# Convolution unrolled with outputs inside its steps, and the choice of experts moved to GpSimd

## The reference, cut to what matters

```python
# second layer, attention part: h = layernorm(x) * (1 + ca) + sa
z = softmax(einsum('bse,he->bsh', h, W_A) * SCALING, axis=1)      # over the sequence, 16 heads
roll = zp[:, :, (i - j) % S] * tril                               # Toeplitz, causal
v = einsum('bse,fe->bsf', h, W_V).reshape(B, S, 16, 8)
out = einsum('bhij,bjhd->bihd', roll, v)
x = x + ga * (out @ W_O.T + b_O)
# second layer, feed-forward part: h = layernorm(x) * (1 + cb) + sb
logits = einsum('bsh,eh->bse', h, gate_w)
w2, i2 = top_k(softmax(logits), 2)
y = relu(einsum('nh,edh->ned', h, expert_w) + expert_b)           # all 16 experts
x = x + gb * sum(take(y, i2) * w2)
```

## Time and profile before

| | us |
|---|---|
| median of 3 runs (1118.16 to 1122.62) | 1119.12 |
| the profiled execution | 1120.54 |
| its span, first to last instruction | 1118.7 |
| TensorE busy in the span | 1036.0 (93%) |
| VectorE busy | 873.4 (78%) |
| ScalarE busy | 844.8 (76%) |
| GpSimd busy | 672.1 (60%) |

### The profile page before, as it was taken

One profiled execution on the slowest core, in us unless ns is written; L12 is line 12 of the kernel. 1 busy time (PEld: TensorE's weight loads), 2 busy tenths in 40 slices (PEclk: granted clock), 3 DMA queues, 4 the chain that ended last, 5 costly groups with the idle time before them and its releaser, 6 DMA issues. The chain is left out here.

```text
span 1118.7 us, 34142 instructions
## 1 busy us (share of the span) xinstructions
PE 1036.0 (93%) x11851; PEld 712.4 (64%) x11851; DVE 873.4 (78%) x2931; ACT 844.8 (76%) x2678; POOL 672.1 (60%) x1080
## 2 busy tenths in 40 slices
PE   6889998799999998998999999998998889999995
PEld 4667764477777776565577777776565588844442
DVE  4999996588888888665688888887676635299998
ACT  5789984699999998433799999997356866488986
POOL 4999995699888887201798898896233300012222
PEclk9999999999999999999999999999999999999999
DMA  7000000112222211311112122121001452000000
GB/s 241 13 3 12 12 3 1 38 41 67 54 55 49 55 44 44 129 50 35 34 40 59 40 49 50 40 50 43 19 1 40 102 146 80 3 11 15 17 18 19
DMA packets 66499, 50.88 MB, mean 45 GB/s; under 512 B 42262, under 2 KB 53442, under 8 KB 66050
## 3 DMA queue, kind: packets, MB, share of 16 engines
q1 hardware_dynamic: 66339, 48.84, 17.1%
HBM read 21.41 MB, written 2.38 MB: 21 GB/s over the span
## 5 line engine op out<-in xcount | busy, mean ns | idle before, releaser
L1259 PE MATMUL psum<-wa_wqkv,wa_hT 128*128 128x512 f32 x384 | 190.1, 603 | 1.3 <-DVE wa_tmp L1124 1.3
L1216 ACT ACTIVATE wa_p<-psum,wa_nb 128x128 f32<-128x128 f32 x512 | 184.6, 403 | 0.0
L1105 POOL TENSOR_TENSOR wa_p<-wa_p,wa_rrs 128x512 f32<-128x512 f32 x128 | 133.4, 1042 | 10.1 <-DVE wa_rrs L1149 10.1
L1812 POOL TENSOR_TENSOR ex_total<-ex_total,mod 128x128 f32<-128x128 f32 x32 | 15.5, 485 | 205.0 <-DVE ex_total L1940 205.0
L1140 DVE CUSTOM_DVE_ANT_0 psum<-psum,wa_bias 128x128 f32<-128x128 f32 x512 | 132.5, 323 | 6.1 <-PE psum L1297 6.1
L1216 ACT ACTIVATION_READ_ACCUMULATOR wa_p<-psum,wa_nb 128x1 f32 x512 | 124.6, 243 | 0.0
L1987 ACT ACTIVATE cv_z_ex_yw<-psum,ex_w 128x128 f32<-128x128 f32 x384 | 107.0, 400 | 19.8 <-DVE ex_w L1916 7.3
L2058 PE MATMUL psum<-ex_wc,ex_hT 128*128 128x512 f32 x256 | 117.7, 603 | 3.5 <-DVE cv_z_ex_yw L1923 2.1
L1081 POOL TENSOR_TENSOR wa_kr<-wa_kr,wa_tmp 128x512 f32<-128x512 f32 x64 | 81.7, 1277 | 41.6 <-DVE wa_tmp L1124 41.6
L1226 ACT ACTIVATE wa_pT<-psum 128x512 f32<-128x512 f32 x128 | 78.3, 612 | 31.9 <-PE psum L1273 31.7
L1092 POOL TENSOR_TENSOR wa_qr<-wa_qr,wa_rn 128x512 f32<-128x512 f32 x64 | 66.8, 1044 | 57.1 <-ACT wa_rn L1198 57.1
(11 more groups left out here) (264 smaller groups left out, 3026.6 us busy)
## 6 DMA issues: line engine op xcount, KB each, us to landing
wa_vm<-wa_v SPq DMA_DIRECT2D x127, 128.0 KB, 2.4
cv_toep<-cv_zpad SPq DMA_DIRECT2D x32, 136.0 KB, 2.7
cv_toep<-cv_zpad SPq DMA_DIRECT2D x16, 264.0 KB, 4.0
wa_tabs<-in_rotations_dram SPq DMA_DIRECT2D x2, 2048.0 KB, 8.1
wa_rows<-y_rows SPq DMA_DIRECT2D x31, 128.0 KB
wa_rows<-y_rows SPq DMA_DIRECT2D x31, 127.0 KB
x_rows<-in_L_attn_x_dram SPq DMA_DIRECT2D x4, 512.0 KB, 6.1
out_dram<-x_rows SPq DMA_DIRECT2D x32, 64.0 KB, 1.5
```

The costliest lines, as they stand in the source:

```text
L1105: nc.gpsimd.tensor_tensor(p, p, cols_bc(rrs[:, t % 2, r, :], P), ALU.mult)\
L1216: e = nc.scalar.activation(pr[:, t % 2, r, h, :], sim_bank[r][:, P * h:P * h + P], ACT.Exp, bias=nb[:, t % 2, r, h:h + 1], scale=-1.0, acc ...
L1259: nc.tensor.matmul(bank, hT[:, t % 3, :], wqkv[:, INNER * k:INNER * k + INNER], start=True, stop=True).then_inc(done.sem, 1)
```

## The change

The convolution's steps are written out, without a loop. The outputs of the first batch are moved into the second batch's steps: the first turn behind step 4, then in each of steps 5 to 7 the projection of one group and the turn of the next, between the second and the third part; the last projection behind step 7. Rounds 10 to 13 of the set-up go into steps 0 and 1, in the same place. The first six tiles are normalised behind the last step instead of during step 4. ScalarE takes the second batch's exponential, the first `values_now` and `lower_rows` ahead of its last two set-up copies. Copies of the values of groups 3 to 7 move from ScalarE to VectorE. `wog`, `bog` and `mixing` move from VectorE to GpSimd, and GpSimd's bias additions wait for the first batch's probabilities and for rows of step 2. In the experts the five stages of the choice move from VectorE to GpSimd; the comparison is now eight instructions of 128x16 instead of one of 128x128.

```diff
         def phase(gp):
+            def floats(g):
+                v_idx.wait(gp, GT * g)
+                nc.gpsimd.tensor_copy(topf[:, g % 2], topi[:, g % 2, :, 0:2]).then_inc(g_float.sem, 1)
+            def numbers_equal(g):
+                g_float.wait(gp, GT * g)
+                for i in range(GT):
+                    for k in range(2):
+                        m = nc.gpsimd.tensor_scalar(equal[:, g % 2, i, k, :], iota[:, :], topf[:, g % 2, i, k:k + 1],
+                                                    None, ALU.is_equal)
+                m.then_inc(g_equal.sem, 1)
...
+            def weights(g):
+                g_masked.wait(gp, GT * g)
+                v_rec.wait(gp, GT * g)
+                for k in (0, 3):
+                    relu_done[k].wait(gp, GT * (g - 2) + GT - 1)
+                nc.gpsimd.tensor_tensor(w[:, g % 2], chosen[:, g % 2], cols_bc(zrec[:, g % 2], NE), ALU.mult)\
+                  .then_inc(g_w.sem, 1)
-            return Phase([(residual, UP_LAG + 2)], 0, TILES)
+            return Phase([of(floats, 5), of(numbers_equal, 5), of(either, 5), of(masked, 6), of(weights, 6),
+                          (residual, UP_LAG + 2)], 0, TILES)
...
-            return Phase([(relu, UP_LAG), of(z_sum, 6), of(numbers_equal, 5), half[0], of(columns, 2), of(top_values, 4),
-                          of(reciprocal, 6), of(either, 5), of(masked, 6), half[1], of(indices, 4), of(weights, 6),
-                          half[2], of(below_top, 4), of(floats, 4), half[3]], 0, TILES, between)
+            return Phase([(relu, UP_LAG), of(z_sum, 6), half[0], of(columns, 2), of(top_values, 4),
+                          of(reciprocal, 6), half[1], of(indices, 4), half[2], of(below_top, 4), half[3]], 0, TILES,
+                         between)
...
             def relu(t):
-                v_w.wait(dve, t)
+                g_w.wait(dve, t)
...
+                on_gpsimd.mixing(gp)
+                gp.wait_ge(g_w, 2)
                 for g in range(GROUPS):
+                    if g % PER_B == 0:
+                        gp.wait_ge(*((v_rec_prob, 2), (v_lower, parts_done(2, 2)))[batch(g)])
...
+                def values(g):
+                    dve.wait_ge(p_zv, 2 * g + 2)
+                    take_values(nc.vector.tensor_copy, g).then_inc(v_v, 1)
...
-                for r in range(1, SET_BEFORE, 2):
+                for r in (1, 3, 5):
                     on_vector.take(dve, r)
-                for r in range(len(PARTS)):
+                lower_rows(0, 0)
+                for r in (7, 9):
+                    on_vector.take(dve, r)
+                for r in range(1, len(PARTS)):
                     lower_rows(0, r)
-                on_vector.add_bias(dve, 0)
                 probabilities(1)
...
+                    if s < 2:
+                        on_vector.take(dve, SET_BEFORE + 2 * s + 1)
+                    if s in (1, 2):
+                        on_vector.add_bias(dve, s - 1)
+                    if s > QUADS:
+                        g = s - QUADS - 1
+                        residual(g)
+                        on_vector.statistics(dve, g, residual_done)
+                        if g:
+                            on_vector.shift(dve, g - 1)
...
-                for b in range(B):
-                    with pe.Fori(0, QUADS // 2) as j:
-                        for u in range(2):
-                            convolve(j + j + (u + QUADS * b), u)
...
+                for s in range(STEPS):
+                    g = s - QUADS
+                    begin_convolve(s)
+                    for r in range(len(PARTS)):
+                        if r == len(PARTS) - 1:
+                            if g > 0:
+                                o_project(g - 1)
+                                turn_o(g)
+                            if s < 2:
+                                for k in range(2):
+                                    on_tensor.prepare(pe, SET_BEFORE + 2 * s + k)
+                        convolve_part(s, s % 2, r)
+                    if g == 0:
+                        for r in range(SET_BEFORE, SET_ROUNDS):
+                            on_tensor.set_over(pe, r)
+                        turn_o(0)
+                o_project(PER_B - 1)
...
-                for r in range(0, SET_BEFORE, 2):
+                for r in (0, 2, 4):
+                    on_scalar.take(act, r)
+                z_exp(1)
+                values_now(0)
+                lower_rows(0, 0)
+                for r in (6, 8):
                     on_scalar.take(act, r)
                 on_scalar.constants_ready(act)
                 act.sem_inc(a_conv, 2)
...
+                o_columns(PER_B - 1)
+                on_scalar.scale(act, PER_B - 2)
                 keep(STEPS - 1)
+                for step in range(EARLY):
+                    phase.step(step)
```

More of the change, by code:

```diff
@@ L1805, in fill, with mixing @@
             nc.gpsimd.memset(rows[:, :, 0:1], 1.0).then_inc(g_set, 1)
+        def mixing(gp):
+            nc.gpsimd.tensor_copy(pick[...], c.ident[:, :]).then_inc(g_mix, 1)
+            gp.wait_ge(g_mix, 1)
+            nc.gpsimd.memset(pick[0:1, :], -1.0).then_inc(g_mix, 1)
+            gp.wait_ge(g_mix, 2)
+            for b in range(B):
+                nc.gpsimd.tensor_scalar(mix[:, b, 1:P], pick[:, 1:P], c.mod_cols[:, 1, CB, b:b + 1], None, ALU.mult)\
+                  .then_inc(g_mix, 1)
+                nc.gpsimd.tensor_copy(mix[:, b, 0:1], c.mod_cols[:, 1, SB, b:b + 1]).then_inc(g_mix, 1)
         def phase(gp):
@@ new lines, in numbers_equal, with either @@
+            def numbers_equal(g):
[5 more added lines that the diff above has]
+                m.then_inc(g_equal.sem, 1)
+            def either(g):
+                g_equal.wait(gp, GT * g)
+                e = equal[:, g % 2]
+                nc.gpsimd.tensor_tensor(chosen[:, g % 2], e[:, :, 0, :], e[:, :, 1, :], ALU.add)\
+                  .then_inc(g_chosen.sem, 1)
@@ L1995, in experts, with prepare @@
     class Tensor:
-        def prepare(pe, r, bank_left=None):
+        def prepare(pe, r):
             if r == 0:
                 pe.wait_ge(loaded, 16 * LOADS)
[L2000 to L2003, removed]
+            for before in range(r):
+                if set_bank(before) is set_bank(r):
+                    set_done(pe, before)
             bank = set_bank(r)
@@ L2117, in convolution_and_experts, with values_taken, take_values @@
         batch = lambda g: g // PER_B
+        ON_VECTOR = 3
+        def values_taken(eng, g):
+            if g < ON_VECTOR:
+                eng.wait_ge(a_v, g + 1)
+            else:
+                eng.wait_ge(v_v, g + 1 - ON_VECTOR)
+        def take_values(instruction, g):
+            to = vall[:, batch(g), 2 * GT * (g % PER_B):2 * GT * (g % PER_B) + 2 * GT, :]
+            return instruction(to, v_bank[g % 2].rearrange("p (n e) -> p n e", e=HALF))
         side = lambda a: slice(HALF * a, HALF * a + HALF)
@@ L2246, in _ @@
                         keep(s - 1)
-                    if s == QUADS:
-                        for g in range(PER_B):
-                            residual(g)
-                            on_vector.statistics(dve, g, residual_done)
                     if s + 1 < STEPS:
@@ L2253, in _ @@
                             lower_rows(s + 1, r)
-                    if s == QUADS:
-                        for g in range(PER_B):
-                            on_vector.shift(dve, g)
-                later = {9: lambda: on_vector.add_bias(dve, 1)}
+                    if s < 2:
[8 more added lines that the diff above has]
+                            on_vector.shift(dve, g - 1)
+                later = {}
                 for k, g in enumerate(range(PER_B, GROUPS)):
@@ L2376, in _ @@
+                o_project(PER_B - 1)
+                for left in conv_left:
+                    left()
+                for step in range(EARLY):
+                    phase.step(step)
+                for g in range(PER_B, GROUPS + 1):
+                    if g < GROUPS:
+                        turn_o(g)
+                        phase.step(EARLY + g - PER_B)
+                    if g > PER_B:
+                        o_project(g - 1)
                 for step in range(EARLY + PER_B, EX_STEPS):
@@ L2454, in _ @@
                         keep(s - 1)
[L2455 to L2457 removed]
+                    if s > QUADS:
+                        o_columns(s - QUADS - 1)
                     if s + 1 < STEPS:
```

200 lines of the change are left out of this document (78 added, 122 removed).

## The result

The changed kernel took 1114.24 us (median of 20 runs, 1110.04 to 1119.45), the kernel before 1119.61 us beside it (20 runs, 1117.24 to 1123.73): ratio 0.9949, 95% interval 0.9937 to 0.996, so 5.7 us less (4.5 to 7.1). The prediction was 1110.5 us.

What follows compares the result with a forecast made beforehand. Bound by TensorE in the convolution's steps, by TensorE and ScalarE waiting on each other between batches and in the lead-in, by VectorE in the experts; -4.4 - 3.4 - 0.8 = -8.6 us from 1119.12 gives 1110.5 us, range 1106 to 1118.

Steps and rivals of the forecast that it cites:

- Set-up: Before step 0 of the second block's convolution: step 0 starts earlier, 0.9 us gained, bounds 0 and 1.7.
- Convolution: Second block's convolution steps: first batch 10.0 us shorter, second batch 6.5 us longer.
- Unrolling itself I cost at nothing: Convolution steps: written-out code costs nothing, since step 0 first ran through its code in the same 7.79 us.
- The gain of the interleaving itself: Between the convolution's batches: 11.7 us there become 7.8 us of pieces in the steps, 3.9 us gained.
- Lead-in: From the convolution's end to the experts' first halving: 3.4 us gained, bounds 2 and 4.5.
- Choice: Experts, choice moved to GpSimd: 0.1 us gained a group, 0.8 us in all, bounds -3.2 and +4.
- first rival: Experts: the choice is free for VectorE, small instructions fit in gaps; -3.2 for -0.8, 1108.1 us; chance 0.15.
- shared reads: Experts: GpSimd's added instructions slow VectorE's halvings by 0.3 us a group, between 0 and 0.9.
- third rival: Convolution: inserted turns wait in each step as between the batches, 4.4 us not gained, 1114.9 us; chance 0.11.
- fourth rival: Experts: GpSimd's chain comes late, every group waits 1.4 us, 1122.5 us; chance 0.12.

Runs made afterwards that it cites:

- the control: The changed kernel run once more, unaltered, against the kernel before: 1113.51 us (11 runs), ratio 0.9942.

## Why the prediction was right and wrong

The direction held and so did the wide range, 1106 to 1118 us; the forecast's own range of 1107 to 1114 was missed by 0.2, and the time isn't below the 1113.5 that the prediction called faster. The gain was two thirds of the forecast, and three of the four terms were off. That the total came so near is in part luck: the convolution was 4.1 us worse than forecast and the lead-in 0.9, the set-up 1.3 better and the experts 2.2.

**Set-up.** Forecast 0.9 us, measured 2.2. Step 0 did not wait for the two set-up copies that ScalarE was still doing:

```profile
881.93 1.09 ACT L1963 ACTIVATE ex_wc<-psum 128x512 f32<-128x512 f32 x2
...
882.52 3.79 PE L2347 MATMUL psum<-cv_v_now,cv_toep 64*64 64x256 f32 x75
```

I had put the wait on `a_conv` behind the copies, because the increment follows them in program order; it took effect 0.5 us before they ended. That made 1.8 of the 2.2 us, just beyond my bound of 1.7; the other 0.4 came from the values' copies, which I had at nothing with a bound of 1.

**Convolution.** Forecast 77.42 to 74.0 us, measured 78.13, in undisturbed profiles of its variants 77.1 to 78.5. The step that failed is "Unrolling itself I cost at nothing". I had argued from step 0, which ran for the first time in 7.79 us, but steps 0 and 1 have waits of 1.76 and 1.69 us ahead of them; in the changed kernel the debt shows from step 3 on. A sign of it stood in the earlier trace rows: the second batch took 32.52 us where four steps and a turn-round of 0.39 make 31.6, with the stall of 0.65 us shown above. I took 31.2 for its steps and so booked that as gained. The weight loads, which TensorE issues first, idle without a wait for 0.50 us ahead of step 3, 1.15 ahead of step 4, 0.22 and 1.33 in it, 0.18 and 0.38 in the steps behind: 3.8 us of the 4.1 missing. The third rival (the inserted turns wait, nothing gained, 1114.9 us) is near the measured time by luck: between part 2 and the turns nothing waits, and what was lost in the convolution was made up elsewhere. The gain of the interleaving itself, 3.9 us by forecast, fell to 0.7 (0.4 to 1.8); steps 4 to 7 ran without a stall where the seam lay ahead of them, which fits a seam that had been giving the instructions time.

**Lead-in.** Forecast 3.4 us, measured 2.5 with the clock at 1.00 (22.85 to 20.38), within the bounds of 2 to 4.5; the first turn started 2.8 us behind the convolution, as forecast. In the profiled run nothing was gained, since the clock fell. I had no price for that, because the earlier trace rows show 1.00 in this stage.

**Choice.** Forecast 0.8 us, measured 3.5; the experts' stage as a whole is 3.0 us shorter, since the rest of the change lengthens it by 0.5 (123.08 with the choice back, 122.61 before). That is near the first rival's 3.2, and a group took 15.70 us, less than the 15.9 that was to be that rival's sign. Both halves of the term were off. The gain I had at 0.4 us a group, before the 0.3 for shared reads; all told it was 0.60. I had charged 0.24 us back, because a halving of 1.46 us had met GpSimd's residual in the earlier trace rows. But with the choice ahead of it in GpSimd's queue the residual meets halvings elsewhere: over 1000 to 1100 us 12 of the 25 1024-wide halvings took 1.45 us before, and 6 of 25 after, and their mean fell from 1350 to 1281 ns. And the shared reads cost VectorE next to nothing: the 512-wide halving rose from 681 to 739 and the 256-wide from 417 to 452, so that the four together took 2765 ns a tile where they took 2738, 0.1 us a group. It is GpSimd that is held: its multiplication rose from 457 to 866, and its comparison took 533 where the nearest row, one in the first layer, had 249. The saving falls in six groups, not eight.

Of the rule in the Trainium skill (SBUF — State Buffer, "Who interferes with whom") the trace bears out the blocking on GpSimd's side. On VectorE's side little of it shows: 22 ns on a halving for eight more comparisons a group. The fourth rival, to which the rule taken in full leaned, did not come in.

**The fourth rival** was a real edge. GpSimd's chain for one group in the changed kernel:

```profile
1037.02 0.31 POOL L1829 CAST ex_topf<-ex_topi 128x8 f32<-128x8 uint32 x1 [2.68 <-DVE ex_topi L1911]
1037.43 4.09 POOL L1835 TENSOR_SCALAR ex_equal<-ex_iota,ex_topf 128x16 f32<-128x16 f32 x8
...
1041.88 1.51 POOL L1823 TENSOR_TENSOR ex_total<-ex_total,mod 128x128 f32<-128x128 f32 x1
...
1044.73 0.36 POOL L1856 TENSOR_TENSOR ex_w<-ex_chosen,ex_zrec 128x64 f32<-128x64 f32 x1
```

The weights end at 1045.09 and the ReLU that reads them starts at 1045.35. With more than 0.3 us added on GpSimd the rival would have come in, as the doubled comparisons showed.

**Sum.** Undisturbed: -2.2 + 0.7 - 2.5 - 3.0 = -7.0 us; the ratio gives -5.7, with an interval of 4.5 to 7.1 that just holds it. The two profiled executions, each with a fall of the clock, were 4.2 and 5.3 us shorter in the block. Falls (2.7 us in the first) and stalls that vary (2.15 us in the control) are enough for the difference. How often each happens in unprofiled runs stays open, as does what starts a fall of the clock.

## What to carry to other kernels

Writing a loop out is not free for an engine that issues 512 short instructions in 7.79 us: leave a stretch that can run from a loop, or one with waits, ahead of the written-out one, and price what runs for the first time, a loop's first pass too. Work moved to a slower engine that shares reads cost the busy engine little here, but price its lateness: compare the time between its input and the next reader with its own operations stretched by what the sharing did to it (here 533 against 249 ns). Where TensorE waits back and forth with another engine or stalls, add the price of a fallen clock as a possibility, even if the trace of before shows none.

## What was new about the hardware

- Written-out products (256 and as many weight loads in 7.79 us) stalled TensorE for 0.2 to 2.2 us at a time without any semaphore, in the changed kernel from the fourth step on, and by no more than 0.4 us where a loop or the seam came first. A loop's first pass lost 0.9 us (16.45 against 15.59), its second nothing.
- An increment of a semaphore on ScalarE took effect 0.5 us before the copies ahead of it in the queue ended.
- With VectorE's two-input additions and GpSimd's small reads side by side, GpSimd's instructions took about twice as long (multiplication 457 to 866 ns, comparison 533 against 249 for the nearest one elsewhere), and VectorE's four additions a tile 27 ns more together (2738 to 2765).
- The same work was granted 1.00 in one execution and 0.50 for some 7 us in another; the first layers alone moved the second block's start over 7 us between profiles.
